# A float32 network on one core: wide attentions that turn their probabilities with a diagonal of inverse sums, a split last output product, and norms shared by two engines

## What is computed

```python
def _L0_xattn_ref(queries, keys, values, Wq, bq, Wk, bk, Wv, bv, Wo, bo):
    B, L, D_MODEL, H, DK, DV = (4, 256, 128, 16, 64, 64)
    ...
    scores = jnp.einsum('blhe,bshe->bhls', q, k)
    causal = jnp.triu(jnp.ones((l, s), bool), k=1)
    scores = jnp.where(causal[None, None], -jnp.inf, scores)
    A = jax.nn.softmax(scale * scores, axis=-1)
    out = jnp.einsum('bhls,bshd->blhd', A, v).reshape(b, l, H * DV)
    return out @ Wo + bo
...
x = x + _L0_xattn_ref(_layernorm(x, axis=-1), ctx_1024, ctx_1024, ...)
x = x + _L0_ffn_ref(_layernorm(x, axis=-1), ...)
x = x + _L1_xattn_ref(_layernorm(x, axis=-1), ctx_1024, ctx_1024, ...)
x = x + _L1_ffn_ref(_layernorm(x, axis=-1), ...)
x = x + _L2_xattn_ref(ctx_1024, _layernorm(x, axis=-1))
x = x + _L2_ffn_ref(_layernorm(x, axis=-1), ...)
x = x + _L3_xattn_ref(_layernorm(x, axis=-1), ...)
x = x + _L3_ffn_ref(_layernorm(x, axis=-1), ...)
```

## Time and profile before

| | |
|---|---|
| median of 3 runs | 1105.91 us (1103.2 to 1107.31) |
| the profiled execution's own time | 1095.65 us |
| its span in the trace | 1093.7 us |
| TensorE busy | 929.4 us (85%) |
| VectorE busy | 687.4 us (63%) |
| ScalarE busy | 476.8 us (44%) |

### The profile page before, as it was taken

One profiled execution on the slowest core, in us unless ns is written; L12 is line 12 of the kernel. 1 busy time (PEld: TensorE's weight loads), 2 busy tenths in 40 slices (PEclk: granted clock), 3 DMA queues, 4 the chain that ended last, 5 costly groups with the idle time before them and its releaser, 6 DMA issues. The chain is left out here.

```text
span 1093.7 us, 18084 instructions
## 1 busy us (share of the span) xinstructions
PE 929.4 (85%) x6590; PEld 584.1 (53%) x6590; DVE 687.4 (63%) x2640; ACT 476.8 (44%) x1123; POOL 2.4 (0%) x15
## 2 busy tenths in 40 slices
PE   4999999899999999999799998166781359899998
PEld 3666666656666666666565656022330243577646
DVE  3656556566656656565665535999999954555353
ACT  3656555555545545555414444322332135313450
POOL 0000000000000000000000000000000000000000
PEclk9999999999999999999998999588955579989999
DMA  8720000000000000000000000000000000000000
GB/s 231 148 63 1 1 1 1 1 1 1 1 1 1 1 1 1 1 1 1 1 1 1 2 1 2 1 1 1 1 0 1 1 2 1 1 1 1 1 1 20
DMA packets 25480, 13.67 MB, mean 12 GB/s; under 512 B 13097, under 2 KB 23729, under 8 KB 25394
## 3 DMA queue, kind: packets, MB, share of 16 engines
q1 hardware_dynamic: 25394, 12.52, 4.6%
HBM read 11.99 MB, written 0.52 MB: 11 GB/s over the span
## 5 line engine op out<-in xcount | busy, mean ns | idle before, releaser
L443 ACT ACTIVATE wide_probs<-PS,wide_nmax 128x512 f32<-128x512 f32 (+2 forms) x256 | 140.2, 556 | 47.7 <-DVE wide_nmax L368 47.7
L368 DVE TENSOR_REDUCE wide_nmax<-PS 128x2 f32<-128x1024 f32 (+2 forms) x128 | 113.6, 888 | 33.1 <-PE PS L313 23.7
L313 PE MATMUL PS<-wide_kT,wide_qT 64*128 64x512 f32 (+2 forms) x512 | 110.2, 507 | 2.1 <-ACT wide_kT L437 2.1
L326 PE MATMUL PS<-constants,wide_probs 128*128 128x128 f32 x704 | 101.3, 278 | 0.0
L93 PE MATMUL PS<-constants 128*128 128x256 f32 x326 | 87.5, 395 | 6.0 <-DVEq L98 6.0
L291 PE MATMUL PS<-wide_pT,wide_v 128*64 128x256 f32 (+1 forms) x768 | 90.2, 370 | 0.2 <-DVE wide_v L363 0.2
L326 PEld LDWEIGHTS PS<-constants,wide_probs 128*128 128x128 f32 x704 | 78.0, 141 | 18.6 <-ACT wide_probs L443 12.0
L449 ACT COPY wide_pT<-PS 128x512 f32<-128x512 f32 (+2 forms) x128 | 57.7, 450 | 45.6 <-PE PS L326 45.6
L1535 PE MATMUL PS<-w_up_or_diagonal,constants 128*128 128x512 f32 (+2 forms) x44 | 27.9, 724 | 50.5 <-DVE w_up_or_diagonal L1691 50.5
L93 PEld LDWEIGHTS PS<-constants 128*128 128x128 f32 x326 | 57.6, 194 | 21.3 <-DVEq L98 8.4
L374 DVE COPY wide_pT<-PS 128x512 f32<-128x512 f32 (+2 forms) x128 | 66.2, 517 | 2.6
(11 more groups left out here) (426 smaller groups left out, 1760.9 us busy)
## 6 DMA issues: line engine op xcount, KB each, us to landing
ctx_by_lane<-ctx_dram SPq DMA_DIRECT2D x4, 256.0 KB, 7.6
top_w<-L_ffn_W_dram SPq DMA_DIRECT2D x2, 512.0 KB
constants<-constants_dram SPq DMA_DIRECT2D x1, 679.0 KB, 5.2
x<-x_dram SPq DMA_DIRECT2D x1, 512.0 KB, 4.1
l0x_wq<-L_xattn_Wq_dram SPq DMA_DIRECT2D x1, 512.0 KB, 9.0
l0x_wk<-L_xattn_Wk_dram SPq DMA_DIRECT2D x1, 512.0 KB, 5.9
l0x_wv<-L_xattn_Wv_dram SPq DMA_DIRECT2D x1, 512.0 KB, 6.8
l0x_bv<-L_xattn_bv_dram SPq DMA_DIRECT2D x1, 512.0 KB, 5.5
```

The costliest lines, as they stand in the source:

```text
L313: mm = pe.matmul(PS[:, self.S[qt][h], 0:self.keys(qt)], w.qT[rows, n % 2, qt * P:qt * P + P], w.kT[rows, n % 2, 0:self.keys(qt)], start=Tr ...
L326: mm = pe.transpose(PS[:, self.T[h], kt * P:kt * P + P], w.probs[:, qt, h, kt * P:kt * P + P], ident)
L368: v.tensor_reduce(w.nmax[:, (2 * n + qt) % 4, :], PS[:, self.S[qt][0]:self.S[qt][1] + 1, 0:self.keys(qt)], AX.X, ALU.max, negate=True).the ...
L443: act.activation(w.probs[:, qt, h, 0:self.keys(qt)], PS[:, self.S[qt][h], 0:self.keys(qt)], ACT.Exp, bias=w.nmax[:, (2 * n + qt) % 4, h:h ...
```

## The change

The inverse sums are applied when the probabilities are turned. For each query tile VectorE inverts the two sums and multiplies the identity by them, which gives two diagonal matrices (`diag`); `turn` multiplies the probabilities by the diagonal where it used to transpose with the identity. Product "t", `repeat`, `take_spread` and the multiplication in `normalise` go; `take_out` is a plain copy. k comes ahead of q, and VectorE takes the maximum ahead of q. The last batch's output product is written to two banks of the scores, seven of its eight parts for the first query tile ahead of the last PV, seven for the second behind it, and the eighth parts at the end.

Of the norms, five are shared: VectorE scales five tiles and evicts the second transposed half, ScalarE scales three (as scale times x plus a shift) and evicts the first. The statistics of the batches that are finished are made inside the block before, where `add_x` is, or in the warping between its two additions; so only two tiles (four after the warping) are left behind the meeting. The norms after the token shift and before l3x still make all eight there. In l1f's program on ScalarE, `scalar_rows` moves behind `scalar_find`. The rest renames semaphores.

```diff
     def scalar_prime(self, act):
 
-        act.activation(self.std[:, 0:1], self.half[:, 0:1], ACT.Sqrt, scale=-1.0).then_inc(self.s_prime, 1)
+        act.activation(self.primed[:, :], self.half[:, 0:1], ACT.Sqrt, scale=-1.0)
 
     def scalar_std(self, act, n):
-        act.wait_ge(self.s_prime, n + 1)
         act.wait_ge(self.s_mv, TILES * (n + 1))
         act.activation(self.std[:, :], self.mv[:, :, 1], ACT.Sqrt, bias=self.k.cst[:, C_EPS:C_EPS + 1]).then_inc(self.s_std, 1)
 
-    def vector_stats(self, v, n, src):
-        for t in range(TILES):
+    def scalar_norm(self, act, n, src):
+
+        act.wait_ge(self.s_rstd, self.rstd_in(n) + 1)
+        for t in range(self.BY_V, TILES):
+            act.activation(self.k.y[:, t, :], src[:, t, :], ACT.Identity, bias=self.shift[:, t - self.BY_V:t - self.BY_V + 1],
+                           scale=self.rstd[:, t:t + 1]).then_inc(self.s_y_act, 1)
+
+    def vector_stats(self, v, n, src, tiles, at):
+
+        for t in tiles:
             v.bn_stats(self.stats[:, t, :], src[:, t, :]).then_inc(self.s_stats, 1)
...
+            v.wait_ge(self.s_stats, TILES * n + at + i + 1)
             v.bn_aggr(self.mv[:, t, :], self.stats[:, t, :]).then_inc(self.s_mv, 1)
 
-    def vector_norm(self, v, n, src, dst):
+    def vector_norm(self, v, n, m, src, dst):
         v.wait_ge(self.s_std, n + 1)
         v.reciprocal(self.rstd[:, :], self.std[:, :]).then_inc(self.s_rstd, 1)
-        v.wait_ge(self.s_rstd, n + 1)
+        v.wait_ge(self.s_rstd, self.rstd_in(n))
         v.wait_ge(self.s_mv, TILES * (n + 1))
-        for t in range(TILES):
+        if m in self.SHARED:
+            rest = slice(self.BY_V, TILES)
+            v.scalar_tensor_tensor(self.shift[:, :], self.mv[:, rest, 0], -1.0, self.rstd[:, rest], ALU.mult, ALU.mult).then_inc(self.s_rstd, 1)
+        for t in range(self.vector_tiles(m)):
             v.tensor_scalar(dst[:, t, :], src[:, t, :], self.mv[:, t, 0:1], self.rstd[:, t:t + 1],
                             ALU.subtract, ALU.mult).then_inc(self.s_y, 1)
 
-    def tensor_transpose(self, pe, n, m):
+    def tensor_transpose(self, pe, m):
 
         for t in range(TILES):
 
-            pe.wait_ge(self.s_y, TILES * n + t + 1)
+            if t < self.vector_tiles(m):
+                pe.wait_ge(self.s_y, self.by_vector(m - 1) + t + 1)
+            else:
...
+    def vector_yT(self, v, m):
+        v.wait_ge(self.s_tps, 2 * m + 2)
+        v.tensor_copy(self.k.yT[:, BANK:2 * BANK], self.k.PS[:, self.TPS[1], :]).then_inc(self.s_yT_v, 1)
...
 
 
-        self.uses = [("q", 0), ("k", 0), ("v", 0), ("q", 1), ("k", 1)]
+        self.uses = [("q", 0), ("k", 0), ("v", 0), ("k", 1), ("q", 1)]
         for n in range(self.PAIRS):
             self.uses += self.first_half(n) + self.second_half(n)
-        self.uses += [("t", self.PAIRS - 1), ("o", self.PAIRS - 1), ("out", B - 1)]
-        self.taken_by = {"q": self.w.q_sb, "k": self.w.k_sb, "v": self.w.v_sb, "t": self.w.sp_sb, "o": self.w.nm, "out": self.x_add,
-                         "w": self.wo_sb}
+        self.uses += [("o", self.PAIRS - 1)]
+        self.taken_by = {"q": self.w.q_sb, "k": self.w.k_sb, "v": self.w.v_sb, "o": self.w.at, "out": self.x_add, "w": self.wo_sb}
 
     def first_half(self, n):
-        return [("t", n - 1), ("o", n - 1)] if n else []
+        return [("o", n - 1)] if n else []
 
     def second_half(self, n):
-        more = [("q", n + 2), ("k", n + 2)] if n + 2 < self.PAIRS else []
+        more = [("k", n + 2), ("q", n + 2)] if n + 2 < self.PAIRS else []
         more += [("v", n + 1)] if n + 1 < self.PAIRS else []
...
                 for kt in range(n_kt):
                     mm = pe.matmul(bank[:, kt * P:kt * P + P], k.ctxT[:, b, kt * P:kt * P + P], self.wv[:, r * P:r * P + P], start=True, stop=True)
                 mm.then_inc(self.w.v_ps, 1)
-            elif kind == "t":
-                pe.wait_ge(self.w.iv, self.n0 + n + 1)
-                for qt in range(QT):
-                    mm = pe.transpose(bank[:, qt * P:qt * P + P], w.inv[:, n % 2, qt, :], ident)
-                mm.then_inc(self.w.sp_ps, 1)
...
 
         def turn(n, qt):
             for h, taken, turned in ((0, self.w.pt_v, self.w.tr_v), (1, self.w.pt_a, self.w.tr_a)):
-                pe.wait_ge(self.w.ex, 4 * (self.n0 + n) + 2 * qt + h + 1)
+                pe.wait_ge(self.w.dg, 2 * (self.n0 + n) + qt + 1)
                 if self.n0 or n or qt:
                     pe.wait_ge(taken, 2 * (self.n0 + n) + qt)
                 for kt in range(self.keys(qt) // P):
-                    mm = pe.transpose(PS[:, self.T[h], kt * P:kt * P + P], w.probs[:, qt, h, kt * P:kt * P + P], ident)
+                    mm = pe.matmul(PS[:, self.T[h], kt * P:kt * P + P], w.probs[:, qt, h, kt * P:kt * P + P],
+                                   w.diag[:, (2 * n + qt) % 4, h, :], start=True, stop=True)
                 mm.then_inc(turned, 1)
 
-        pe.wait_ge(k.ln.s_yT, self.yT_in)
+        def last_output(qt, rows):
+
+            out = PS[:, self.S[0][qt], 0:P]
+            for i in rows:
+                mm = pe.matmul(out, w.attT[:, i, qt * P:qt * P + P], self.wo[:, i, :], start=(i == 0), stop=(i == 7))
+            return mm
+
...
             for u in self.second_half(n):
                 product(u)
-        for u in (("t", self.PAIRS - 1), ("o", self.PAIRS - 1), ("out", B - 1)):
-            product(u)
+        pe.wait_ge(self.w.at, self.n0 + self.PAIRS - 1)
+        last_output(0, range(7))
+        product(("o", self.PAIRS - 1))
+        last_output(1, range(7))
+        pe.wait_ge(self.w.at, self.n0 + self.PAIRS)
+        last_output(0, (7,))
+        last_output(1, (7,)).then_inc(self.w.out_ps, 1)
 
     def vector(self, v):
         k, w, PS = self.k, self.w, self.k.PS
...
-        def invert(n):
-            v.wait_ge(self.w.ex, 4 * (self.n0 + n) + 4)
-            v.reciprocal(w.inv_few[:, :, :], w.sums[:, n % 2, :, :]).then_inc(self.w.iv_few, 1)
-
-        def repeat(n):
-            v.wait_ge(self.w.iv_few, self.n0 + n + 1)
-            v.tensor_copy(w.inv[:, n % 2, :, :].rearrange("p t (h f) -> p t h f", h=2),
-                          w.inv_few[:, :, :].unsqueeze(3).to_broadcast((P, QT, 2, 64))).then_inc(self.w.iv, 1)
-
-        def normalise(n):
-            v.wait_ge(self.w.sp_sb, self.n0 + n + 1)
+        def invert(n, qt):
+
+            at = (2 * n + qt) % 4
+            v.wait_ge(self.w.ex, 4 * (self.n0 + n) + 2 * qt + 2)
+            v.reciprocal(w.inv[:, at, :], w.sums[:, n % 2, qt, :]).then_inc(self.w.iv, 1)
+            v.wait_ge(self.w.iv, 2 * (self.n0 + n) + qt + 1)
+            v.tensor_tensor(w.diag[:, at, :, :], k.ident.unsqueeze(1).to_broadcast((P, 2, P)),
+                            w.inv[:, at, :].unsqueeze(2).to_broadcast((P, 2, P)), ALU.mult).then_inc(self.w.dg, 1)
+
+        def take_out(n):
             v.wait_ge(self.w.av, self.n0 + n + 1)
-            v.tensor_tensor(w.attT[:, n % 8, :], PS[:, self.bank(("o", n)), 0:L], w.spread[:, n % 2, :], ALU.mult).then_inc(self.w.nm, 1)
...
         def add_x(b):
+            v.wait_ge(self.x_add, b + 1)
+            if b:
+                k.ln.vector_stats(v, self.norm_next, k.x, range(QT * b - QT, QT * b), QT * b - QT)
             v.wait_ge(self.w.out_ps, self.n0 // 8 + b + 1)
-            v.wait_ge(self.x_add, b + 1)
-            v.tensor_tensor(k.x[:, 2 * b:2 * b + 2, :], k.x[:, 2 * b:2 * b + 2, :],
-                            PS[:, self.bank(("out", b)), 0:L].rearrange("p (t d) -> p t d", t=QT), ALU.add).then_inc(self.x_add, 1)
+            out = PS[:, self.bank(("out", b)), 0:L].rearrange("p (t d) -> p t d", t=QT) if b < B - 1 else PS[:, self.S[0][0]:self.S[0][1] + 1, 0:P]
+            v.tensor_tensor(k.x[:, 2 * b:2 * b + 2, :], k.x[:, 2 * b:2 * b + 2, :], out, ALU.add).then_inc(self.x_add, 1)
 
         v.wait_ge(self.wqk_in, 64)
         take_q(0)
...
         take_v(0)
+        invert(0, 0)
         take_q(1)
         v.tensor_tensor(k.x[:, :, :], k.x[:, :, :], self.bo[:, :].unsqueeze(1).to_broadcast((P, TILES, P)),
                         ALU.add).then_inc(self.x_add, 1)
         for n in range(self.PAIRS):
             take_turned(n, 0)
+            invert(n, 1)
             if n + 1 < self.PAIRS:
                 maximum(n + 1, 0)
             if n:
-                normalise(n - 1)
+                take_out(n - 1)
             take_turned(n, 1)
-            invert(n)
+            if n + 1 < self.PAIRS:
+                invert(n + 1, 0)
+                maximum(n + 1, 1)
             if n + 2 < self.PAIRS:
                 take_q(n + 2)
-            repeat(n)
             if n + 1 < self.PAIRS:
-                maximum(n + 1, 1)
                 take_v(n + 1)
             if self.wo_by_head and n == 2:
                 take_wo(0)
                 take_wo(1)
             if n >= 8 and n % 8 == 0:
                 add_x(n // 8 - 1)
-        normalise(self.PAIRS - 1)
...
 
         def add_x(b):
+            v.wait_ge(self.x_add, b + 1)
```

(28 more changed lines are left out.)

170 lines of the change are left out of this document (95 added, 75 removed).

## The result

The changed kernel takes **1173.16 us** (median; 1171.0 to 1176.42), the kernel before 1104.56 us (1097.92 to 1107.31) on the same chip: 1.065 times as long, with a 95% interval of 1.060 to 1.071. The forecast was 1164 us. In the profiled executions the span goes from 1093.7 to 1173.5 us, 79.8 us more; that is 11 us more than the 68.6 between the medians. The execution of before that was profiled was a quick one (1095.65 us), which accounts for 8.9 of the 11.

A forecast was written before the change was run, and what follows sets the result against it. TensorE instructions were taken to bound both wide attentions, so added ones are paid in full. The terms 78.1 - 19.2 + 12.6 - 2.1 - 3.0 - 8.4 gave +58 us on the median 1105.91, so 1164 us; range 1143 to 1176.

The forecast's parts named there:

- turn: Both wide attentions: each turned tile takes two TensorE instructions instead of one, 704 added at 0.111 us, +78.1 us.
- The wait for the diagonal: Turns of both wide attentions: the wait for exponents, reciprocal and diagonal fits into the slack, cost 0.
- last output: End of each wide attention: splitting the output products around the last PV gains 1.5 us each, -3.0 us together.
- product t: Both wide attentions: dropping the small product that spreads the inverses saves 0.30 us in each of 64 pairs, -19.2 us.
- order and wait, l1x: Second wide attention: v now waits for ScalarE's taking of k, about 0.42 us in 30 pairs, +12.6 us.
- order, l0x: First wide attention: v starts 1.15 us after k instead of 1.23 after q, -2.1 us over 30 pairs.
- norms: Norms between stages: earlier statistics and scaling shared with ScalarE shorten them, -8.4 us in all.
- a single instruction per tile: Turn of the wide attentions: the diagonal product issues like a transpose, the turn costs nothing more, 1086 us; chance 0.05.
- hidden slack: TensorE's slots are long from hidden waits, half the added instructions fit into them, +19 us, 1125 us; chance 0.05.
- a wait that doesn't open: Second wide attention: q's slot and the switches fill v's new wait, +45 us, 1151 us; chance 0.14.
- Rival 3: First wide attention: the diagonal is late by 0.3 us per pair, 10 us more, 1174 us; chance 0.08.

The follow-up runs named there:

- experiment 5: The kernel before with every transpose of a wide turn issued twice, without a diagonal: 1176.34 us beside 1100.25 (ratio 1.071).
- experiment 2: The changed kernel with q before k again on TensorE and q taken ahead of the maximum on VectorE: 1151.41 us (ratio 1.046 to the kernel before).
- experiment 1: The changed kernel turning with identity transposes again, diagonals still made and waited for but unused: 1090.41 us beside 1100.66 for the kernel before (ratio 0.988).

## Why the prediction was off

The main steps of the forecast held, a doubled turn and a new wait of v in l1x, and the sizes of both costs were too small. The order was short by 5.7 us in l1x, the turn by 5.1. The wait for the diagonal, which was put at nothing, cost 1.9; in the table it is part of the last output (0.75) and of the rest (1.15). By its own terms, in us, measured from the starts in the profile (l1x 32 pairs, l0x 32 pairs, 30 of each with k and q):

| term | forecast | measured |
|---|---|---|
| turn | +78.1 | +83.2 (32 x 1.87 + 32 x 0.73) |
| product t | -19.2 | -18.9 |
| order and wait, l1x | +12.6 | +18.3 (30 x 0.61) |
| order, l0x | -2.1 | -0.6 |
| last output | -3.0 | -3.3 (-1.4, -1.9; from the last turn to the meeting, less what the turn itself grew) |
| norms | -8.4 | -6.9 (1.9 + 1.9 + 1.5 + 1.6, behind l0x, l1x, l1f and l3x) |
| rest, not foreseen | 0 | +8.0 |
| sum | +58 | +79.8 in the profiles; +68.6 by the medians |

**The turn** was the right mechanism, and its price per instruction was nearly right: I took 0.111 from v, two transposes have 0.109, a product in this place 0.117. It lies between v's row and the upper bound of 0.127 that I had from the turn's own slots. The rivals of a single instruction per tile and of hidden slack fall with x16 and with experiment 5. The rival of a wait that doesn't open falls with v's 0.35 us in each of 30 pairs.

By the Trainium skill, page "Perfetto Trace Analysis", section "Transposes", logical transposes are to be done as transposes; the trace agrees, 0.97 us against 1.88 for the same eight tiles. The factor of 4 for FP32 in the Trainium skill, page "TensorE: Matmul & The Clock Gate", section "Terms", is not what these runs show for a turned tile; it is 1.9.

**The order** is the step that failed most by size: 0.61 us per pair of l1x where I had 0.42. I put 1.80 us between k and v, it is 1.90: the switch behind the scores, which was paid by q's slot (0.54 for half the columns of k's 0.86), is now paid by k (0.96), and ScalarE gets k 0.10 later (1.16 after its start, 1.06 before). And I stopped counting at v's start. Behind the wait, v's eight instructions take 1.00 and not 0.89; experiment 2 takes the wait away and has 0.89 back, experiment 1 keeps it and keeps 1.00. Together 0.08 to 0.10 and 0.11 for 30 pairs are the 5.7 us that are missing in l1x. In l0x I expected 0.07 from the new order and found 0.02.

**The diagonal** was made in 0.425 us (0.43 forecast). In steady pairs it was never late, as forecast. It was late twice, where I had not looked: 1.15 us in the first pair of l0x, behind the addition to x, and 0.75 us at the end of l0x, where nothing is queued ahead of the turn and which ate part of the split output's gain. Rival 3, a diagonal late by 0.3 us in every pair of l0x, did not come; that its 1174 us lie next to the measured 1173 is chance.

**The norms** behind l0x and l1x and ahead of l3f gave 1.8, 1.9 and 1.6 (1.8 forecast for each), the one ahead of the warping 1.5 (1.6 forecast). Sharing alone gave 0.3 where I had 0.5, behind the token shift and ahead of l3x (there in the traces whose 18 products took the short form, 5.78 from the meeting against 6.06). The one behind the warping gave nothing where I had 0.4. In the part l1f the gain shows only between traces of the same granted clock: at 0.95 it takes 147.2 us with the old norm and 145.2 and 145.5 with the new one, at 0.93 149.9 and 147.9.

**The rest:** l1f is 2.7 us longer than its shorter norm would make it, l2f 1.4, l3x 2.5; l0x some 2 beyond its terms. Of these 2 us, 1.15 are the diagonal's wait in the first pair, and in 0.7 the first v starts later (22.35, before 21.64; it lies between 21.24 and 22.35 in the traces of kernels with the new norms, so this is scatter between executions). The first three show a lower granted clock in some stretch, at other places in each execution, and so are no effect of the change that these runs can show.

Adding the sum to the median was sound. Without the rest the measured terms add up to 71.8 us, which is 13.8 more than the 58 of the forecast: the order is short by 7.2 of them (5.7 in l1x, 1.5 in l0x), the turn by 5.1 and the norms by 1.5, while t and the last output cancel. The medians give 68.6; the 3 us between lie within what they scatter.

## What to carry to other kernels

Before a scale is folded into a transpose, count instructions on the engine that bounds: here a float32 product is two where a transpose is one, and the 704 more cost more than the 64 small products that went could give back. If TensorE is full and the others stand near two thirds, scale the operand on them ahead of the transpose, and look at the first and the last pair, where nothing hides that work. Before something is made to wait for an engine, read what that engine does just ahead of it at the start of the stage, not only in a steady pair. When a product moves to another place, price its switch there and let the count run to the end of the group behind the wait, not to its start.
